# Convolution in half-width column tiles, two moved image shifts, and routing products in 32-column tiles: first stage of a routed-convolution and scan kernel

## The reference

```python
for t in range(3):                                    # STEPS
    k, v = x @ Wk, x @ Wv                             # 2 heads of 16
    attn = softmax(q . k / 4, over the 1024 pixels)
    logits = (sum over pixels of attn * v) @ Wmlp     # 4 experts
    attn_map = attn.mean(over heads)
    weights = softmax(where(allowed, logits, -1e9) / 1.5)
    wsel = the two largest weights, normalised, the others 0
    x_mod = x * (1 + attn_map * 1024 * softplus(alpha))
    x = sum over e of wsel[e] * (conv3x3(x_mod, We[e]) + be[e])
    allowed = allowed without the top expert (the last one stays)
```

## Time and profile before

| | us |
|---|---|
| median of 3 runs | 3929.95 |
| lowest and highest | 3929.83, 3930.94 |
| the profiled execution, its time | 3930.42 |
| its span (first to last instruction) | 3928.6 |
| first stage, until the last convolution product | about 692 |

### The profile page before, as it was taken

How to read it: one execution, slowest core, us unless ns; L and a number is a source line. 1 busy time by engine, 2 the same in 40 slices (tenths; PEclk the granted TensorE clock), 3 DMA queues, 4 the chain that set the end, 5 groups by cost and what they waited for, 6 DMA issues and landing times. The chain is left out here.

```text
span 3928.6 us, 34661 instructions
## 1 busy us (share of the span) xinstructions
PE 3689.2 (94%) x8780; PEld 1491.8 (38%) x8780; DVE 3742.5 (95%) x3409; ACT 2928.7 (75%) x4422; POOL 3273.4 (83%) x1542
## 2 busy tenths in 40 slices
PE   7999999899999999999999999999999999999998
PEld 3444444333333333333333333333333333333333
DVE  6778787999999999999999999999999999999998
ACT  3454554888888888888888888888888878888885
POOL 2221222799999999999999999999999999999998
PEclk9999999999999999999999999999999999999999
DMA  4142324889999989999989999999899998999986
GB/s 113 34 123 59 114 66 136 320 343 347 354 354 348 349 347 351 347 348 346 347 348 347 354 355 348 349 348 350 347 348 347 345 348 350 353 351 348 349 342 255
DMA packets 203160, 1181.08 MB, mean 301 GB/s; under 512 B 30961, under 2 KB 31761, under 8 KB 68817
## 3 DMA queue, kind: packets, MB, share of 16 engines
q1 hardware_dynamic: 200128, 1177.64, 79.4%
q10 hardware_dynamic: 2832, 1.23, 0.1%
HBM read 1144.03 MB, written 34.73 MB: 300 GB/s over the span
## 5 line engine op out<-in xcount | busy, mean ns | idle before, releaser
L1547 POOL TENSOR_TENSOR read<-state,bc_all 128x1024 f32<-128x1024 f32 x1024 | 2395.5, 2362 | 109.0 <-DVE state L1611 108.9
L1611 DVE TENSOR_TENSOR_SCAN state<-decays,p_drive 128x1024 f32<-128x1024 f32 x1024 | 2289.6, 2274 | 18.9 <-ACT p_drive L1446 5.5
L1316 PE MATMUL p_y<-read,ident 128*128 128x512 f32 x4096 | 1955.6, 604 | 16.1 <-POOL read L1547 8.7
L1438 ACT ACTIVATE decays<-dt,wa 128x496 f32<-128x496 f32 x2048 | 1337.0, 702 | 75.3 <-DVE state L1611 72.9
L1316 PEld LDWEIGHTS p_y<-read,ident 128*128 128x128 f32 x4096 | 739.6, 190 | 1053.4 <-issue 772.5
L1598 DVE TENSOR_TENSOR p_drive<-bc_all,p_dtx 128x1024 f32<-128x1024 f32 x768 | 909.0, 1215 | 0.0
L1564 POOL TENSOR_TENSOR pool_drive<-dtx,bc_all 128x1024 f32<-128x1024 f32 x256 | 603.3, 2356 | 3.0 <-DMA bc_all<-bc_scratch 2.8
L766 POOL TENSOR_TENSOR pad<-map_all,xc 128x512 f32<-128x512 f32 x96 | 139.4, 1482 | 521.0 <-DMA map_all<-map_scratch 457.2
L1446 ACT COPY p_drive<-pool_drive 128x1024 f32<-128x1024 f32 x256 | 260.8, 1019 | 414.6 <-DVE state L1611 414.6
L1312 PE MATMUL p_y<-xconv,d_diag 128*128 128x512 f32 x256 | 143.9, 644 | 156.4 <-DVE gated L1621 156.4
L556 PE MATMUL p_conv<-pad,wm 128*128 128x512 f32 x576 | 269.3, 603 | 2.7 <-issue 2.0
(11 more groups left out here) (162 smaller groups left out, 3106.4 us busy)
## 6 DMA issues: line engine op xcount, KB each, us to landing
bc_all<-bc_scratch SPq DMA_DIRECT2D x1024, 1024.0 KB, 6.9
map_all<-map_scratch SPq DMA_DIRECT2D x48, 512.0 KB, 5.6
norm_rows<-xn SPq DMA_DIRECT2D x32, 280.0 KB, 5.8
norm_in<-norm_rows SPq DMA_DIRECT2D x64, 140.0 KB, 7.8
norm_in<-norm_rows SPq DMA_DIRECT2D x64, 139.8 KB, 8.1
fresh<-in_x SPq DMA_DIRECT2D x32, 256.0 KB, 6.8
x<-in_x SPq DMA_DIRECT2D x32, 256.0 KB, 3.3
mid_x<-x SPq DMA_DIRECT2D x32, 256.0 KB, 6.5
```

Of the source, the lines that this page charges most:

```text
L1316: nc.tensor.matmul(p_y[:], ident[:], read[:, s % DEEP, :], start=False, stop=(s == N - 1)).then_inc(y_added, 1)
L1438: nc.scalar.activation(decays[:, s % DEEP, :].rearrange("p (q t) -> p q t", t=SIDE)[:, :, 1:], dt[b][:, :, 1:], ACT.Exp, scale=wa[m][:, s: ...
L1547: nc.gpsimd.tensor_tensor(read[:, s % DEEP:s % DEEP + 2, :], state[:, s % DEEP:s % DEEP + 2, :], bc_all[s // CHUNK][:, :, 1, :], ALU.mult) ...
L1611: nc.vector.tensor_tensor_scan(state[:, at:at + 2, :].rearrange("p s n -> p (s n)"), decays[:, at:at + 2, :].rearrange("p s n -> p (s n)") ...
```

## The change

It has four parts, all in the first stage.

1. The main convolution is issued for each dx as two calls of 64 weight columns, one for each output row parity, which write PSUM partitions 0 to 63 and 64 to 127 of the same bank.
2. The anti part is laid out anew: for either output parity, the moving tile `shifted[par]` holds the neighbouring row in its own half and the same row moved by one pixel in the other half, so that one call of 128 input rows covers two of the three dx, and a second call the third (its other 64 rows of weights are zero). Two calls of 64 columns for each parity, four an image in place of three of 128. The mixed weights shrink from 768 to 640 columns (MIX = 384 + 256). The shift becomes four copies an image, and `shifted` is no longer doubled over the two groups: a shift waits for the convolution of the phase before.
3. The shifts of images 2 and 3 leave the end of ScalarE's slot and go into the next slot, behind the exponential and the first `step_out`.
4. `score` issues two calls of 32 weight columns for each image in place of one of 128: rows 0 to 31 and 64 to 95 of `p_route` for images 0 and 1, rows 32 to 63 and 96 to 127 for images 2 and 3.

The loads of the expert weights, the zeroing of the unused quarters and of the border rows, and the order of tiles in memory follow from these.

```diff
-MAIN, ANTI = 3 * 128, 3 * 64
+MAIN, ANTI = 3 * 128, 4 * 64
+MIX = MAIN + ANTI
...
+        def anti_of(rows, out_par, n):
+            at = MAIN + 128 * out_par + 64 * n
+            return we_sb[rows, :, at:at + 64]
+        def tap_of(rows, dx):
+            return we[rows, :, MAIN + 64 * dx:MAIN + 64 * dx + 64]
...
+        for out_par, straight, crossed in ((0, high, low), (1, low, high)):
+            expert_loads += [(anti_of(straight, out_par, 0), tap_of(straight, 1)), (anti_of(straight, out_par, 1), tap_of(straight, 2)),
+                             (anti_of(crossed, out_par, 0), tap_of(straight, 0))]
...
         for dx in range(3):
-            nc.tensor.matmul(bank[:], w_mixed[g][a][:, 0, dx, :], padded[g][a][:, :, dx:dx + SIDE],
-                             start=(dx == 0), stop=False)
+            for par in two:
+                nc.tensor.matmul(bank[CH * par:CH * par + CH, :],
+                                 w_mixed[g][a][:, 128 * dx + CH * par:128 * dx + CH * par + CH],
+                                 padded[g][a][:, :, dx:dx + SIDE], start=(dx == 0), stop=False)
...
-        for dx in range(3):
-            mm = nc.tensor.matmul(bank[:], w_mixed[g][a][:, 1, dx, :], shifted[g][a][:, :, dx:dx + SIDE],
-                                  start=False, stop=(dx == 2))
+        for n in two:
+            for par in two:
+                at = MAIN + 128 * par + CH * n
+                mm = nc.tensor.matmul(bank[CH * par:CH * par + CH, :], w_mixed[g][a][:, at:at + CH],
+                                      shifted[par][a][:, :, 1 + n:1 + n + SIDE], start=False, stop=(n == 1))
...
-            mm = nc.tensor.matmul(p_route[:], route[:, 128 * a:128 * a + 128], xc[g][a][:], start=(a == 0), stop=(a == TEAM - 1))
+            for part in two:
+                at = R * part + R // 2 * (a // 2)
+                mm = nc.tensor.matmul(p_route[at:at + R // 2, :], route[:, 128 * a + at:128 * a + at + R // 2],
+                                      xc[g][a][:], start=(a % 2 == 0), stop=(a % 2 == 1))
...
-        ge(act, conv_done, 4 * (P - 2) + a + 1)
+        ge(act, conv_done, 4 * (P - 1) + a + 1)
         act.wait_ge(padded_ready, 4 * P + a + 1)
-        nc.scalar.copy(shifted[g][a][0:64, 0:ROWS2 - 1, :], padded[g][a][0:64, 1:, :])
-        nc.scalar.copy(shifted[g][a][64:128, 1:ROWS2, :],
-                       padded[g][a][64:128, :ROWS2 - 1, :]).then_inc(shifted_ready, 1)
+        for par, source, there, here in ((0, slice(64, 128), slice(1, ROWS2), slice(0, ROWS2 - 1)),
+                                         (1, slice(0, 64), slice(0, ROWS2 - 1), slice(1, ROWS2))):
+            crossed = slice(64 * par, 64 * par + 64)
+            nc.scalar.copy(shifted[par][a][source, there, 1:], padded[g][a][source, here, 1:])
+            o = nc.scalar.copy(shifted[par][a][crossed, there, 1:], padded[g][a][source, here, :SIDE + 1])
+        o.then_inc(shifted_ready, 1)
...
             if steps:
                 step_out(i, k - 1, 0)
+            if P:
+                shift(act, P - 1, 1 - g, 2)
+                shift(act, P - 1, 1 - g, 3)
             if norm:
                 group_root(act, norm[0])
...
             shift(act, P, g, 0)
             shift(act, P, g, 1)
-            if after:
-                shift(act, P, g, 2)
-                shift(act, P, g, 3)
```

More of the change, by code:

```diff
@@ L58, in build @@
         gain = sb("gain", [128, 4])
-        we_sb = sb("we_sb", [128, EXPERTS, 2 * MAIN])
+        we_sb = sb("we_sb", [128, EXPERTS, MIX])
         be_sb = sb("be_sb", [128, EXPERTS])
@@ L104, in build @@
         dve_chain = sem("dve_chain")
-        def anti_of(rows, half, e):
-            return we_sb[rows, e, MAIN:].rearrange("p (d c) -> p d c", d=3)[:, :, 64 * half:64 * half + 64]
+        low, high = slice(0, 64), slice(64, 128)
+        def anti_of(rows, out_par, n):
[3 more added lines that the diff above has]
+            return we[rows, :, MAIN + 64 * dx:MAIN + 64 * dx + 64]
         first_loads = [(wk_sb[:], wk), (q_sb[:], q.partition_broadcast(128)), (wv_sb[:], wvT), (wmlp_sb[:], wmlp),
@@ L111, in build @@
         expert_loads = [(be_sb[:], be), (we_sb[:, :, 0:MAIN], we[:, :, 0:MAIN])]
-        for par in range(2):
-            rows = slice(64 * par, 64 * par + 64)
-            for e in range(EXPERTS):
-                expert_loads.append((anti_of(rows, 1 - par, e), we[rows, e, MAIN:].rearrange("p (d c) -> p d c", d=3)))
+        for out_par, straight, crossed in ((0, high, low), (1, low, high)):
+            expert_loads += [(anti_of(straight, out_par, 0), tap_of(straight, 1)), (anti_of(straight, out_par, 1), tap_of(straight, 2)),
+                             (anti_of(crossed, out_par, 0), tap_of(straight, 0))]
         mamba_loads = []
@@ L245, in _ @@
             nc.vector.memset(route[:], 0.0).then_inc(dve_chain, 1)
-            for e in range(EXPERTS):
-                for par in range(2):
-                    nc.vector.memset(anti_of(slice(64 * par, 64 * par + 64), par, e), 0.0)
+            nc.vector.memset(anti_of(low, 0, 1), 0.0)
+            nc.vector.memset(anti_of(high, 1, 1), 0.0)
             s1["norm_first"](dve)
@@ L339, in stage1 @@
     R = TEAM * 4 * HEADS * 2
-    ZEROS, ZEROS_DVE = 2 * TEAM * 3, 2 * TEAM * 2 + 2
+    ZEROS, ZEROS_DVE = 2 * TEAM * 3, 2 * TEAM + 2
     def sb(name, shape, dt=f32):
@@ L354, in stage1 @@
         padded.append([sb(f"pad_{g}{a}", [128, ROWS2, SIDE + 2]) for a in team])
-        shifted.append([sb(f"shf_{g}{a}", [128, ROWS2, SIDE + 2]) for a in team])
-        w_mixed.append([sb(f"wm_{g}{a}", [128, 2, 3, 128]) for a in team])
+        w_mixed.append([sb(f"wm_{g}{a}", [128, MIX]) for a in team])
         if g == 0:
-            mix0 = [sb(f"mix0_{b}", [128, 768]) for b in two]
+            mix0 = [sb(f"mix0_{b}", [128, MIX]) for b in two]
+            scrap = sb("scrap", [R, PIX])
+            mod_w = sb("mod_w", [R, 128])
+            sb("spare", [128, 1760])
+            shf_00 = sb("shf_00", [128, ROWS2, SIDE + 2])
             map_all = sb("map_all", [128, TEAM, PIX])
@@ L361, in stage1 @@
             attn, map_rows = attn_map[0:R, :], attn_map[R:R + 2 * TEAM, :]
-            scrap = sb("scrap", [R, PIX])
-            mod_w = sb("mod_w", [R, 128])
+    for par in two:
+        shifted.append([shf_00 if a == par == 0 else sb(f"shf_{par}{a}", [128, ROWS2, SIDE + 2]) for a in team])
     for g in two:
@@ L842, in mix_last @@
         ge(dve, conv_done, 4 * (P - 2) + a + 1)
-        nc.vector.scalar_tensor_tensor(w_mixed[g][a][:].rearrange("p m d c -> p (m d c)"), c["we"][:, 3, :],
+        nc.vector.scalar_tensor_tensor(w_mixed[g][a][:], c["we"][:, 3, :],
                                        wsel[:, a, 3:4], mix0[a % 2][:], ALU.mult, ALU.add).then_inc(w_ready, 1)
@@ L853, in norm_first @@
         norm_scale(dve, 0)
-        for g in two:
-            for a in team:
-                nc.vector.memset(shifted[g][a][0:64, ROWS2 - 1, :], 0.0).then_inc(zeroed_dve, 1)
-                nc.vector.memset(shifted[g][a][64:128, 0, :], 0.0).then_inc(zeroed_dve, 1)
+        for a in team:
+            nc.vector.memset(shifted[0][a][:, 0, :], 0.0).then_inc(zeroed_dve, 1)
+            nc.vector.memset(shifted[1][a][:, ROWS2 - 1, :], 0.0).then_inc(zeroed_dve, 1)
     def last_vector(dve, part):
```

## The result

The changed kernel takes 3886.49 us (median of 4 runs) against 3929.89, a ratio of 0.989 with a 95% interval of 0.9878 to 0.9902: 43 us less. The span of its profiled execution is 3884.5 us, 44.1 under the 3928.6 of before.

What follows compares the result with a forecast made beforehand. TensorE was taken to bound the plain phases, VectorE the dense ones. From 3930 us, 33 less over 23 periods and 4 more at the hand-over gave 3901; own range 3888 to 3918, range on record 3886 to 4012.

Steps and rivals of the forecast that it cites:

- forecast case: First stage: column tiles run entirely parallel, TensorE needs 22.9 us a phase, 3.2 under now; 3901 us, chance 0.45.
- the ring: Loop from main convolution through softmax, mixes, modulation map, DMA and GpSimd's product back; 25.2 us, to become 24.7, bounding plain phases.
- Units: TensorE, each phase: 96 records in parallel column tiles make 46 units of 0.43 us, 19.7 us.
- Switches: TensorE changing tile width: 0.16 us a switch, 1.0 us a phase, bounds 0.3 and 1.9.
- The waits of the kernel before: Four periods of a body exceed 26.07 us because TensorE waits, mostly for VectorE's last mixing step, "wm", 20.0 us.
- the dense phases: Second and third periods of a body: VectorE is the bound, loses 1.6 us, giving 26.6 and 26.1 us.
- Opening: First 50 us: expert loads, memory layout and fewer memsets change nothing within 2 us either way.
- Hand-over: Last phase's doubled shifts on ScalarE delay the copy of bc_rows that opens the second stage: +4 us.
- (1) order kept: TensorE starts matmuls in program order, so 55 units against 56, 26.7 us a phase; 3930 us, chance 0.25.
- (2) loads open: Tiles overlap but weight loads wait for running matmuls, 0.28 us a record, 30.0 us a phase; 4009 us, chance 0.12.
- (3) no overlap: Column tiles run one after another, 96 units, 44.5 us a phase; 4355 us, chance 0.18.
- Cover of the shifts behind the exponential: ScalarE's idle time absorbs 5.05 us of moved shifts at zero cost; 1 us short would cost 24 us.

Runs made afterwards that it cites:

- par_major: Changed kernel with the main convolution's six half-width calls issued as three for even rows, then three for odd, instead of alternating: 3914.5 us.
- anti_major: Changed kernel with the anti convolution's four calls issued as two for even rows, then two for odd, main convolution still alternating: 3885.22 us.
- narrow_before: Kernel before with the four mixing steps of each image over 640 columns instead of 768, TensorE's work unchanged: 3917.25 us.
- map_first: Changed kernel with ScalarE's modulation map copy moved ahead of the second output copy: 3880.60 us.
- early_swap: Kernel of map_first with TensorE's swap product ahead of image 0's anti convolution and one first mixing step, not two, ahead of neg_top: 3904.0 us.
- score_full: Changed kernel with the routing product back at one full-width call of 128 columns an image: 3887.28 us.
- map_first_before: Kernel before with ScalarE's modulation map copy moved ahead of the second output copy: 3929.78 us.
- tiles32: Changed kernel with both convolution parts in four column tiles of 32 in place of two of 64: 3890.0 us.
- shifts_home: Changed kernel with the shifts of images 2 and 3 back at the end of ScalarE's slot: 3978.43 us.

## Why the prediction was right, and where its sizes were off

**Direction and mechanism: right. The size: off, and inside the range by little.** The forecast case came true: tiles work side by side, and TensorE falls under the ring in the plain phases. The gain is 43 us where 29 were predicted (3901). The measured 3886.5 lies 1.5 us below the forecast's own range (from 3888) and 0.5 us above the lower end of the range on record (3886), and one of the four executions, 3884.56, lies outside it. That it stayed inside is luck. The own range's upper end, 3918, is not worked out either: 1 us in each of 23 periods would give 3924.

**Units: right.** There are 46 parallel units a phase. The main part takes 2.57 us, the anti part 1.7, and the routing of three images 1.84 to 1.96 with its switch. The condition was finer than stated: each tile works ahead of the program only so far as four records of its neighbour (par_major, anti_major), and the order in which the calls are written keeps within that. No run has the new anti part on the kernel before by itself, so how the gain divides between units and narrower mixes is known only from the side of the mixes (narrow_before, 12 us).

**Switches: right.** They were put at 0.16 from the one product of the earlier trace rows and measured 0.10 to 0.20.

**The waits of the kernel before: misread.** The prediction took "wm" as the first real releaser of TensorE and the excess of four periods over 26.07 as TensorE held up by it. The earlier trace rows is the list of the weight loads. The matmuls' own list, over the same 60 to 650 us, has:

```profile
PE p_conv L556 <- DVE wm L843: 0.7, 1, 0.7
```

The periods of 26.82 and 26.40 have TensorE busy for 26.79 and 26.40 us, with the products of the group statistics in them, and narrow_before, with less work on VectorE, still has 26.40.

**The phases one by one.** The 22 phases were put at 32 us less (8.7 a body) and gave 39.9. By kind (the place of a period in its body, 1 to 6), with the plain ones of the first body at 24.7 too, the predicted periods sum to 556.6 us and the measured ones to 549.2:

| kind of period (how many) | predicted | measured, mean | sum of the difference |
|---|---|---|---|
| first (3) | 25.4 | 25.9 | +1.6 |
| second, dense (3) | 26.6 | 25.9 | -2.0 |
| third, dense (3) | 26.1 | 25.2 | -2.7 |
| fourth (3) | 25.1 | 24.6 | -1.4 |
| plain, and the first body's four (10) | 24.7 | 24.4 | -3.0 |

So the mis-sized term is, for more than half, that of the dense phases. In the second kind VectorE is the bound as forecast, but how long it takes depends on one thing that the sum left out. Its last mixing pair takes 1.67 us when it is over before GpSimd's four products begin, and 2.69 or 3.73 when it runs beside them. VectorE's timeline, in a plain phase and in two phases of the second kind:

```profile
289.87 1.67 DVE L862 SCALAR_TENSOR_TENSOR wm<-we_sb,wsel,mix 128x640 f32<-128x640 f32 x2
```

```profile
192.49 2.69 DVE L862 SCALAR_TENSOR_TENSOR wm<-we_sb,wsel,mix 128x640 f32<-128x640 f32 x2
```

```profile
343.26 3.73 DVE L862 SCALAR_TENSOR_TENSOR wm<-we_sb,wsel,mix 128x640 f32<-128x640 f32 x2
```

The first of these two phases lasts 25.60 us and the second 26.64, which is that difference. GpSimd's four products take 6.30 and 6.37 us there and 4.95 to 4.98 where the pair is over before them; in the kernel before the pair takes 3.98 instead of 1.94. No run separates the two, so that they slow each other is a reading of which rows coincide, and why they would is not shown. The trace of the exchange alone (map_first) has 3.72 or 3.73 in every phase of the second kind and 26.62 or 26.63 us for each, which is the 2.0 us that it lost there. The third kind is not bound by VectorE at all: in the phase that ends at 377.39, VectorE idles 2.32 us ahead of the maximum and TensorE 1.10 us ahead of the main convolution, as in a plain one.

In the plain phases the ring is 0.3 us shorter than the prediction's two terms (0.8 less, 0.3 more) make it. I have not taken that apart. early_swap shows that the ring has a second leg through TensorE's own queue, swap, sum and modulation behind anti and main parts; the anti part there got shorter by two units, which the sum left out. That this is the missing 0.3 us is only argued.

**Opening.** It was put at nothing within 2 us, and in this pair of traces it gave 4.5. One part is shown: 16 border memsets became 8 of both halves at once, and VectorE's next work starts at 15.68 us where it started at 17.54. The narrower routing products look like another part. TensorE's timelines, before and after:

```profile
20.72 5.72 PE L592 MATMUL p_route<-xc,route 128*128 128x512 f32 x8 [7.93 <-DVE route L276]
```

```profile
18.87 3.44 PE L607 MATMUL p_route<-xc,route 128*32 128x512 f32 x16 [6.09 <-DVE route L282]
```

But score_full, which undoes them, has its first swap 3.2 us later (26.38 against 23.15) and its second only 0.5 later (52.40 against 51.91). In between, the first main convolution takes 4.22 us in the changed kernel, with 0.64 of the clock granted, and 2.73 in score_full, with 1.00:

```profile
44.69 4.29 PE L566 MATMUL p_conv<-pad,wm 128*64 128x512 f32 x12 [1.97 <-issue]
```

```profile
46.75 2.80 PE L566 MATMUL p_conv<-pad,wm 128*64 128x512 f32 x12 [0.58 <-issue]
```

The kernel before has this too: its first main convolution takes 4.35 us in its own trace and 2.65 in that of map_first_before, whose second swap is 1.1 us earlier (55.27). So whether that one convolution runs at the lower level of the clock is worth about a microsecond at the second swap, in either kernel, and the routing products give 0.5 of the 4.5 us there. How the rest divides is not shown.

**Hand-over.** It was put at +4 and measured +0.2. The copy of bc_rows comes 31.7 us after the last swap in the new kernel (632.81) and 28.4 in the old one (645.45 to 673.80), so the doubled copies do delay it by 3.3 us. Five operations later ScalarE takes a product of TensorE out of PSUM, and there the delay is gone. ScalarE's timelines, before and after:

```profile
681.23 0.59 ACT L1410 COPY dt<-p_b 128x512 f32<-128x512 f32 x1 [4.38 <-PE p_b L1292]
```

```profile
636.93 0.58 ACT L1428 COPY dt<-p_b 128x512 f32<-128x512 f32 x1 [1.22 <-PE p_b L1310]
```

Both are 35.8 us after the last swap. ScalarE had 4.38 us of idle time ahead of this copy and now has 1.22. VectorE's first scan, behind it, starts 50.1 us after the last swap in both kernels (695.57 and 651.25). The step that failed took a delay on ScalarE for a delay of the stage without asking what is waited for behind it.

**Rivals.** (1) order kept: excluded by par_major's loads and matmuls. Its 26.7 us a phase should be 26.8 (55 x 0.43 + 3.17), which changes nothing. (2) loads open and (3) no overlap: excluded by the trace after and by tiles32. **Cover of the shifts behind the exponential:** put at zero cost, with 0.2 us to spare in plain phases and about nothing beside the group root; the trace has 0.31 us, and 0 to 0.62 beside the root, and shifts_home shows what a lack of cover costs. In the first and second kinds a shift does hold TensorE, for 0.20 to 1.39 us ahead of the anti convolution of image 0, where the prediction had 1.2; as it said, VectorE is the bound there. No plain phase has such a wait.

## What to carry to other kernels

A product of which a block is zero can be packed into column tiles when the moving data may differ from tile to tile: the gain is in units saved, not in width, and full-width neighbours lose only the switches. Write the calls so that tiles alternate, or at least so that no tile gets more than four records in a row. Before crediting an engine's relief, find the next ring and its length in the same phase: of 3.2 us taken off TensorE a phase, 1.8 arrived, and a copy moved by one place on an engine with time to spare was then worth 6 us, while it had been worth nothing. And look at every kind of phase: the exchange of early_swap was judged by the plain ones and lost most of its 23 us in the others.

## What the runs showed of the hardware that was not expected

- TensorE works ahead across column tiles: in par_major a load of L578 began 0.06 us ahead of one of L566 that stands before it in the program, and their matmuls likewise. The reach lies at four records of a tile, one running and three waiting: four in a row cost nothing (anti_major), six cost two units (3.63 us with a switch instead of 2.72).
- Two fp32 tiles of 64 columns run at twice the rate (12 records in 2.57 us) and four of 32 at four times (24 records in 2.57 us), with weight loads of one row group overlapping each other (four in 0.20 us). The Trainium skill (TensorE: Matmul & The Clock Gate, The mechanism) has matmuls in strict program order and loads overlapping only where the row group differs; neither holds for these column tiles, and the measurements decide.
- A switch of tile width costs 0.10 to 0.20 us.
- Two mixing steps of VectorE (640 columns, fp32) that take 1.67 us by themselves took 2.69 or 3.73 us beside GpSimd's products of 512 columns, and four of these 6.1 to 6.5 us instead of 4.97 (all 22 phases between second and last swap).
